# Laying out the matrices and the transposed input of a DeltaNet and mixture-of-experts layer by partition

## The reference

```python
q = l2norm(silu(causal_conv4(x @ Wq.T)))      # same for k; v without the norm
beta, gamma, mix = sigmoid(x @ Wb.T), sigmoid(x @ Wdec.T), sigmoid(x @ Wmix.T + mix_bias)
o_d = delta_rule_chunkwise(q, k, v, beta)     # state S of 256x256 for each head, token after token
ema = scan(s = gamma * s + (1 - gamma) * v)
o   = rms_norm((1 - mix) * o_d + mix * ema) * onorm_w
x   = layernorm(x + o @ Wo.T)

probs = softmax(x @ choice_w.T)               # 8 experts
G, I  = top_k(probs.T, 512)                   # each expert takes 512 tokens
h     = silu(x[I] @ w1[e])                    # 1024 -> 2048
out   = zeros.at[I].add(G * (h @ w2[e]))      # 2048 -> 1024
x     = layernorm(x + out)
```

## Time and profile before

| | us |
|---|---|
| median of 3 runs | 1215.92 |
| profiled execution, own time | 1218.1 |
| its span on the slowest core (core 4) | 1216.5 |
| spans of the other cores | 1196.7 to 1213.8 |
| PE busy | 1043.6 (86%) |
| mean granted TensorE clock, core 4 | 0.945 |

### The profile page before, as it was taken

How to read it: one execution, slowest core, us unless ns; L and a number is a source line. 1 busy time by engine, 2 the same in 40 slices (tenths; PEclk the granted TensorE clock), 3 DMA queues, 4 the chain that set the end, 5 groups by cost and what they waited for, 6 DMA issues and landing times.

```text
span 1216.5 us, 23626 instructions; the slowest of 8 cores (1196.7 to 1216.5 us)
## 1 busy us (share of the span) xinstructions
PE 1043.6 (86%) x7559; PEld 575.5 (47%) x7559; DVE 542.8 (45%) x1197; ACT 534.1 (44%) x967; POOL 339.6 (28%) x513
## 2 busy tenths in 40 slices
PE   2888995989998999988993179999999999999992
PEld 0454563556655666645552134444444444444441
DVE  3256662676667666657765712212121212100263
ACT  1355663656665666757875022222222222222253
POOL 2013233443334333323223013313131313131035
PEclk9999996999999999989997579999999999999997
DMA  9976797898779877754478919998989898988695
GB/s 233 131 157 136 160 150 165 155 193 187 173 169 188 194 172 171 161 150 151 164 258 297 240 36 143 207 199 185 201 187 199 184 197 197 190 196 212 201 353 206
DMA packets 106981, 226.50 MB, mean 186 GB/s; under 512 B 8565, under 2 KB 52597, under 8 KB 106864
## 3 DMA queue, kind: packets, MB, share of 16 engines
q0 software_dynamic: 66736, 118.24, 56.9%
q1 hardware_dynamic: 40128, 106.76, 25.9%
HBM read 227.89 MB, written 75.50 MB: 249 GB/s over the span
## 4 chain that ended last, share of the span: by engine, by line
PE 69%; DMA 12%; issue 6%; DVE 5%; POOL 3%; ACT 3%; SPq 1%; DVEq 0%; POOLq 0%; ACTq 0%
PE ps L1376 16%; PE ps L1397 16%; PE ps L509 12%; PE ps L556 4%; DMA AR<-w 4%; PE ps L1045 4%; DMA w<-AR 3%; DMA AR<-accd 2%; DMA AR<-wqT 2%; PE ps L772 2%; PE ps L784 1%; PE ps L593 1%; PE ps L865 1%; PE ps L774 1%; DVE AR L1244 1%
## 5 line engine op out<-in xcount | busy, mean ns | idle before, releaser
L1376 PE MATMUL ps<-AR 128*128 128x512 bf16 x1024 | 234.5, 381 | 11.1 <-ACT AR L1468 11.1
L1397 PE MATMUL ps<-AR 128*128 128x512 bf16 x992 | 218.8, 379 | 0.0
L509 PE MATMUL ps<-AR 128*128 128x512 bf16 x768 | 185.9, 390 | 0.9 <-ACT AR L568 0.9
L1397 PEld LDWEIGHTS ps<-AR 128*128 128x128 bf16 x992 | 95.7, 98 | 110.7
L1484 ACT ACTIVATE AR<-ps 128x512 bf16<-128x512 f32 x128 | 76.1, 597 | 159.6 <-PE ps L1376 158.5
L1376 PEld LDWEIGHTS ps<-AR 128*128 128x128 bf16 x1024 | 92.9, 97 | 111.9 <-issue 14.9
L1468 ACT ACTIVATE AR<-ps 128x1024 bf16<-128x1024 bf16 x32 | 32.8, 1024 | 230.4 <-PE ps L1324 230.4
L509 PEld LDWEIGHTS ps<-AR 128*128 128x128 bf16 x768 | 75.1, 101 | 80.2 <-issue 10.5
L827 ACT ACTIVATE AR<-ps 128x512 bf16<-128x512 f32 x160 | 86.7, 597 | 31.5 <-PE ps L774 31.5
L1434 DVE TENSOR_SCALAR AR<-ps,gcol 128x512 f32<-128x512 f32 x48 | 33.8, 747 | 144.6 <-PE ps L1397 144.6
L545 DVE CAST AR<-ps 128x512 bf16<-128x512 f32 x96 | 66.5, 693 | 57.3 <-PE ps L509 54.9
(11 more groups left out here) (184 smaller groups left out, 1673.8 us busy)
## 6 DMA issues: line engine op xcount, KB each, us to landing
AR<-w POOLq DMA_DIRECT2D x72, 512.0 KB, 8.2
w<-AR SPq DMA_DIRECT2D x72, 512.0 KB, 5.0
AR<-w POOLq DMA_DIRECT2D x36, 1024.0 KB, 20.6
AR<-w SPq DMA_DIRECT2D x28, 1024.0 KB, 24.8
AR<-hs SPq DMA_DIRECT2D x16, 512.0 KB, 5.5
accd<-AR SPq DMA_DIRECT2D x16, 512.0 KB, 3.8
AR<-accd SPq DMA_DIRECT2D x16, 512.0 KB, 11.6
x1s<-AR SPq DMA_DIRECT2D x16, 256.0 KB, 2.8
```

The lines of the kernel that those rows point to most:

```text
L509: mm = T.matmul(ps[:, 0:512], w[:, kk, 128 * (i % 2):128 * (i % 2 + 1)], g.hs_fm[b][:, 512 * kk:512 * (kk + 1)], start=(kk == 0), stop=(kk ...
L1376: mm = T.matmul(ps[:, 0:512], w1[:, kk, 128 * (m % 4):128 * (m % 4 + 1)], xe[:, KTOP * kk:KTOP * (kk + 1)], start=(kk == 0), stop=(kk == 7))
L1397: mm = T.matmul(pss[nh][:, 0:512], g.h_fm[kk][:, 128 * tm:128 * (tm + 1)], w2[:, kk % 4, 512 * nh:512 * (nh + 1)], start=(kk == 0), stop=( ...
```

## The change

The host lays out each matrix and the transposed input in another order, and the kernel declares the DRAM tensors in that order. Up to now a transfer into 128 partitions gathered for each partition several separate runs from DRAM: 8 runs of 2 KB for a block of `hsT`, 8 of 1 KB for a head's slice of Wq, Wk or Wv, 8 of 512 B for `wsT`, 8 of 4 KB for `woT`, 8 of 32 B for `cwT`, 8 of 2 KB for a quarter of w1 (8 of 1 KB from `w116`), 4 of 2 KB for a quarter of w2. Afterwards it is one run for each partition: 16 KB, 8 KB, 4 KB, 32 KB, 256 B, 16 KB (8 KB from `w116`) and 8 KB. The bytes, the buffers in SBUF, the number and the order of all instructions, and all waits stay as they are.

The pieces of the cast through the bounce buffers keep the length of their runs (8 KB of float32 read, 4 KB of bf16 written for each partition) but lie otherwise in DRAM: before, the runs of the 128 partitions of one piece followed each other without a gap; afterwards a piece is one half of each partition's row, with 16 KB from run to run when it is read and 8 KB when it is written.

```diff
-    dram("hsT", [D, S])
-    dram("wqT", [D, D])
...
+    dram("hsT", [4, 128, 4096])
+    dram("wqT", [4, 128, 2048])
...
+    dram("wsT", [128, 1024])
+    dram("woT", [128, 8192])
+    dram("cwT", [128, 64])
+    dram("w1", [E, 4, 128, 4096])
+    dram("w2", [E, 4, 128, 4096])
...
-    dram("w216", [E, FF, D], "Internal", BF16)
-    dram("w116", [D, FF], "Internal", BF16)
+    dram("w216", [E, 4, 128, 4096], "Internal", BF16)
+    dram("w116", [4, 128, 4096], "Internal", BF16)
@@ load_w1
-    P.dma_start(out=g.w1r[Q % 6].rearrange("p (kk q) -> p kk q", kk=8),
-                in_=(g.w1[e] if e > 0 else g.w116)[:, 512 * q:512 * (q + 1)].rearrange("(kk p) q -> p kk q", p=128)
+    P.dma_start(out=g.w1r[Q % 6],
+                in_=(g.w1[e] if e > 0 else g.w116)[q]
@@ load_w2
-    X.dma_start(out=g.w2r[Q % 6].rearrange("p (kk q) -> p kk q", kk=4),
-                in_=src[e][512 * q:512 * (q + 1), :].rearrange("(kk p) q -> p kk q", p=128)
+    X.dma_start(out=g.w2r[Q % 6],
+                in_=src[e][q]
@@ chunk_of
-    if x < 8:
-        return w1[128 * x:128 * (x + 1), :]
     e, j = divmod(x - 8, 8)
-    return w2[e][256 * j:256 * (j + 1), :].rearrange("(p r) m -> p (r m)", r=2)
+    return (w1 if x < 8 else w2[e])[j // 2][:, 2048 * (j % 2):2048 * (j % 2 + 1)]
@@ sp_first
-        Y.dma_start(out=g.st_hs[:, 2048 * j:2048 * (j + 1)].rearrange("p (kk t) -> p kk t", kk=4),
-                    in_=g.hsT[512 * j:512 * (j + 1), 0:512].rearrange("(kk p) t -> p kk t", p=128)).then_inc(d.sem, d.up())
+        Y.dma_start(out=g.st_hs[:, 2048 * j:2048 * (j + 1)],
+                    in_=g.hsT[0][:, 2048 * j:2048 * (j + 1)]).then_inc(d.sem, d.up())
...
-        Y.dma_start(out=st.rearrange("p (kk m) -> p kk m", kk=8),
-                    in_=w[:, 0:256].rearrange("(kk p) m -> p kk m", p=128)).then_inc(d.sem, d.up())
+        Y.dma_start(out=st,
+                    in_=w[0]).then_inc(d.sem, d.up())
@@ pool_weights, pool_hs, pool_wo and the load of wsT in pool_program: in the same way
...
+def by_rows(a, *splits):
+
+    r, c = a.shape
+    n, w = splits
+    return np.ascontiguousarray(a.reshape(r // (128 * n), n, 128, c // w, w).transpose(0, 3, 2, 1, 4)).reshape(
+        r // (128 * n) * (c // w), 128, n * w)
@@ host_in_map
-        "hsT": np.ascontiguousarray(hs.T),
+        "hsT": by_rows(hs.T, 8, 512),
...
+        "w1": np.stack([by_rows(a, 8, 512) for a in np.asarray(inputs["L0_ffn_w1"], f32)]),
+        "w2": np.stack([by_rows(a, 4, 1024) for a in np.asarray(inputs["L0_ffn_w2"], f32)]),
```

## The result

| | before | after |
|---|---|---|
| median of 7 runs, us | 1215.5 | 1221.73 (1219.63 to 1224.87) |
| ratio, 95% interval | 1 | 1.0055 (1.0036 to 1.0074) |
| profiled execution, own time, us | 1218.1 | 1222.4 |
| span of the slowest core, us | 1216.5 (core 4) | 1220.8 (core 0) |
| span, mean over the 8 cores, us | 1207.1 | 1207.4 |

The 1215.5 of before are the three runs from above with four more. Ratios and intervals leave out the slow executions, most of them with a lower granted clock on the cores of one die.

The account below looks back on a forecast made before the run. TensorE was busy 86%, with transfers waited for at the start, two bounce stretches and the end. Gains 4.5 + 0.8 + 0.4 = 5.7 us took 1218.1 to 1212.4, or 1210.2 from the median 1215.92; range 1202 to 1219.

Parts of the forecast that it names:

- The start: Loads up to Wq's landing: 6.05 MB at 331 GB/s instead of 266, gain 4.5 us, bounds 0 and 5.9 or 8.
- over 310: Sign to look for: the transfer rate from 5 to 19 us, 281 GB/s before, would be over 310.
- little at the start: Rival, start: memory read by all 8 cores sets 281 GB/s; only 1.2 us less, 1214.7; chance 0.22 with "nothing".
- the unevenness of 1.2 MB: Start: faster engines had begun 1.2 MB of later loads before Wq landed; left unchanged in the 4.5 us.
- woT: Bounce stage, load issued at 154.03 us: 14.0 us for 14.8, gain 0.8 us, bounds 0 and 14.6.
- POOL's other loads: Casting loads of hsT blocks and head slices: not faster for longer runs, and covered; gain nothing.
- The pieces of the bounce: Cast loads and stores as half rows: same bytes and run length, partial-row reading not slower; cost nothing.
- the 78 us of chain that I had named: Bounce stretches at 152.93 to 202.84 and 483.21 to 521.33 us, less 10 for woT; 0.78 us per per cent longer.
- at twice the length: Within rival "slower": only with pieces this long is the four-buffer stretch caught too, losing tens of us.
- slower: Rival, bounce pieces: half-row addresses use fewer memory channels; at 16% longer 6.8 us slower, 1222.7; chance 0.14.
- The experts: Expert stage: shorter transfers lie under TensorE, gain nothing; first gather to last scatter stays at 430 us.
- The scatter: End: last scatter, sharing engines with two w2 quarters, shrinks from 7.68 us by 0.4; bounds 0 and 1.

Follow-up runs that it names:

- e1: The kernel before with long runs only for SP's transfers of the start and wsT; ratio to before 0.9957.
- e2: The changed kernel with expert weights and their copies as before, so only attention inputs in long runs; ratio to before 0.9931, median 1207.43 us.
- e5: The gapless kernel: the changed kernel with bounce pieces without gaps (copies, w2 and expert 0's w1 in eighths); ratio to before 0.9948.
- e8: The gapless kernel e5 with gaps after each piece's runs: 8 KB of each 12 KB read, 4 KB of each 6 KB written; ratio to before 0.9964.
- e9: As e8 with rows of 4096 elements: 8 KB of each 16 KB read, 4 KB of each 8 KB written, gaps empty; ratio to before 1.0052.
- e6: The changed kernel with pieces still read as half rows but written without gaps (copies in eighths); ratio to before 0.9978.
- e7: The changed kernel with pieces read without gaps (w2, expert 0's w1 in eighths) but written as half rows; ratio to before 1.0036.

## Why the prediction was wrong

**The start: nearly the right time, by two errors that cancel.** Forecast were 4.5 us at 331 GB/s. The slowest core shows 3.8 to Wq, the mean of the cores 4.4 to the first projection. But 300 GB/s came in 5 to 19 us, for "over 310", and up to the landing of Wq it was 280 for 264 (the stretch of before, then of after, columns as in the earlier trace rows):

```profile
2.00:24.75 22.75, 3.57 (x8) 1.05 (x8) 7.21 (x9) 3.19 (x2) 2.99 (x4) 1.00 1.01 264
```

```profile
2.00:20.99 18.99, 2.34 (x6) 0.87 (x7) 7.22 (x9) 3.19 (x2) 3.16 (x6) 1.00 1.00 280
```

The 6.0 MB of before take 21.4 us at 280 GB/s, only 1.3 less, which is what the rival "little at the start" said (1.2). The other 2.5 us come from this: only 5.3 MB had been moved when Wq landed. That is the unevenness of 1.2 MB which I had left "as it is"; 0.7 MB of it are gone. So the rate was forecast far too high and this term at nothing, and that the sum fits was luck. What follows moved along with the start, as said, and e1 shows that the gain lasts: 0.43%, or 5.2 us.

**woT: a wash instead of 0.8 us.** In e2 the fifth transfer of that place is issued 3.8 us earlier than before, of which the start accounts for about 4. woT itself lands 22.9 us after its issue for 25.5 (means over the cores, after and before), but the store beside it is longer by as much as the next load is shorter.

**POOL's other loads: nothing was granted.** e2 against e1 is 0.26% in the ratios, with overlapping intervals, and 4.4 us in the mean first gather (686.4 for 690.8), which is no more than this differs between kernels that are alike up to there. A gain is possible and not shown.

**The pieces of the bounce: here it failed.** The step read "reading a part of each row is not slower there. I take nothing". The row behind it was a read, hsT with 2 KB of every 8 KB at 157 GB/s, compared with pieces at 150. For reading it was wrong by little: half rows cost 0.3% when read, at the edge of what is told from nothing. I carried it over to writing, where no row of the trace had the pattern, and writing half rows costs 0.9%. By the medians over the cores a store took 5.16 us for 4.76 and a load 8.11 for 7.89. Together that is 5% on a round trip, and on the 78 us of chain that I had named it makes 4 us. Against the gapless kernel, whose neighbours are the same (4.72 and 7.55 us), it is 8%, and 6 us. But there are two new places too, near 240 and 371 us: with longer round trips four buffers no longer cover the pieces behind the slices of heads 2 and 3 (24 us of waits in 220 to 460 us, for 9 in e5). I had counted those as covered and had let the cover go only "at twice the length". With them the pieces' part of the loss is 1.1% (changed against gapless), or 13 us. The rival "slower" had the pattern, its place and its sign, with a chance of 0.14. Its price per per cent was too low, since it took the stretches on the chain for fixed.

The Trainium skill's rule that I cited for this rival (DMA: Bandwidth & Descriptors, section "Latency and other measured facts", pitch at large powers of two) names pitches from 512 KiB on. Here 8 and 16 KB suffice, and its two remedies work here as well: a pitch that is larger than the run by a few KiB and no power of two (e8 against e9), and tiles laid out contiguously (e5). The cause that it gives, streams that fall on the same channels of memory, is an inference there and remains one here: no row shows channels. The shortest store takes 2.6 us in both kernels and only the median is longer, so a store is not slower by itself; which neighbours make it so, no run tells.

**The experts: right, but for the end.** The chain of after has the first gather and the last scatter here, which answers to the earlier trace rows:

```profile
707.27 3.82 DMA AR<-x1s,idxc
...
1138.13 9.11 DMA accd<-AR,idxc
```

That is 430.9 us for 430.3. The scatter got longer there and not shorter (9.11 us for 7.68, where 0.4 less were forecast), and the 2.2 us behind the last issue were in no row of before.

**The sum.** Attention inputs -0.69% (e2), pieces +0.3% and +0.9% (e6 and e7 against e5), end +0.2% (2.2 us): +0.7%, measured +0.55%. The longest new bar of the profile was harmless, and the loss came for the most part from some 0.4 us more on the median of 72 stores and what followed from it.

## What to carry to other kernels

When a layout is changed for the sake of one reader, follow every transfer that touches the tensor, and look at the distance from run to run and at its length: here a store of 4 KB of every 8 KB, by all partitions at once, cost twice as much as long runs at the start gave. Lay each transfer's destination out without gaps, or keep the distance off a power of two (shown here for 6 and 12 KB alone). A wait that several buffers cover has a margin; find how large it is before a small slowdown behind it is priced by its present share of the chain. And what is shown for reading is not shown for writing.

## What I had not expected of the hardware

The 28 casting loads of w1 by POOL, when they have runs of 16 KB of float32, leave 2.2 us more between the last issue and the end of the program, 9.7 to 10.0 for 7.2 to 7.7 us, on each of 8 cores in each of nine kernels with them; with w1 in runs of 8 KB or 2 KB it is not there, although three early loads of hsT with 16 KB and one of woT with 32 KB still are.

The casting load of woT in one queue, with runs of 32 KB, holds up a store in the other until it has landed itself: in the changed kernel woT lands at 175.4 us and the store at 175.6. On the slowest cores the store beside woT takes 17.6 to 20.3 us in the kernels with these long runs and 8.9 to 9.9 in those with runs of 4 KB. And yet the time from the first to the fifth transfer of this place stays (38.9 us in the changed kernel, 38.1 in e2, 38.8 before); the DMA engines were busy all the time from 156 to 175 us.
